# Attention step of a layer kernel: TensorE issues the first pair of scores ahead of the step's first bank of maxima

## What is computed

```
xn  = layernorm(x)
out = x + attention(xn) + experts(xn)

attention: 16 sub-heads of 8 features for q and k, 8 heads of 16 features for v
  q = rope(xn Wq.T) * 8**-0.5,  k = rope(xn Wk.T),  v = xn Wv.T
  probs = softmax(q k.T)                      # 16 x 1024 x 1024 per batch
  diff  = probs[even] - lam * probs[odd]
  y     = rms_normalise(diff v) * (1 - 0.36) ; y Wo.T
experts: 3 of 8 zones per batch, chosen by a router on the mean token:
  sum of w[e] * gelu(xn Wa[e]) Wb[e]
```

## Time and profile before

| | us |
|---|---|
| median of 3 runs | 438.38 (437.73 to 438.41) |
| the profiled execution | 437.34 |
| its span, first to last instruction | 435.6 |
| TensorE busy | 413.3 |
| VectorE busy | 384.4 |
| ScalarE busy | 338.8 |

### The profile page before, as it was taken

One profiled execution on the slowest core, in us unless ns is written; L12 is line 12 of the kernel. 1 busy time (PEld: TensorE's weight loads), 2 busy tenths in 40 slices (PEclk: granted clock), 3 DMA queues, 4 the chain that ended last, 5 costly groups with the idle time before them and its releaser, 6 DMA issues.

```text
span 435.6 us, 7697 instructions
## 1 busy us (share of the span) xinstructions
PE 413.3 (95%) x2742; PEld 185.1 (42%) x2742; DVE 384.4 (88%) x743; ACT 338.8 (78%) x450; POOL 141.4 (32%) x172
## 2 busy tenths in 40 slices
PE   8899999999999899999999999999999999999983
PEld 6665556655565333333332333333333333345542
DVE  4995999999999899999999999899999998888476
ACT  3786565555554799989889989989989899888971
POOL 4269999878763500111020010120121210000002
PEclk9999999999999999999999999999999999999998
DMA  8736751400000150020002063000000000000003
GB/s 273 289 97 216 242 199 47 140 9 1 3 0 3 29 216 0 13 87 3 2 3 98 1 150 49 1 2 2 2 3 0 3 0 4 2 2 2 4 0 96
DMA packets 21871, 24.94 MB, mean 57 GB/s; under 512 B 11818, under 2 KB 16106, under 8 KB 21578
## 3 DMA queue, kind: packets, MB, share of 16 engines
q1 hardware_dynamic: 21096, 23.60, 17.1%
q10 hardware_dynamic: 738, 0.86, 0.7%
HBM read 14.49 MB, written 8.65 MB: 53 GB/s over the span
## 4 chain that ended last, share of the span: by engine, by line
PE 62%; ACT 13%; DVE 13%; issue 9%; DMA 1%; POOL 1%; ACTq 0%; POOLq 0%; DVEq 0%
PE ps L1399 17%; PE ps L1252 16%; ACT E L795 10%; PE ps L1362 10%; DVE part_max L905 6%; PE ps L1324 4%; PE ps L1177 3%; PE ps L1179 3%; PE ps L1178 2%; PE ps L1325 2%; PE ps L1326 2%; PE ps L1390 1%; DMA X<-in_x 1%; PE ps L1380 1%; DVE stats L859 1%
## 5 line engine op out<-in xcount | busy, mean ns | idle before, releaser
L905 DVE TENSOR_REDUCE part_max<-ps 128x1 f32<-128x512 f32 x512 | 319.9, 680 | 28.7 <-PE ps L1252 24.6
L795 ACT ACTIVATE E<-ps 128x1024 f32<-128x1024 f32 x256 | 245.4, 1029 | 32.3 <-PE ps L1362 27.6
L1399 PE MATMUL ps<-E,Vg 128*32 128x512 f32 x896 | 119.3, 604 | 0.1
L1252 PE MATMUL ps<-K,Q 32*128 32x512 f32 x384 | 111.4, 473 | 0.6
L1252 PEld LDWEIGHTS ps<-K,Q 32*128 32x128 f32 x384 | 46.7, 182 | 84.7 <-DVE part_max L905 76.0
L1362 PE MATMUL ps<-Q,K 32*128 32x512 f32 x320 | 77.9, 480 | 4.7 <-ACT E L795 3.1
L559 POOL TENSOR_TENSOR hL<-h,hH 128x512 fp32r<-128x512 f32 x48 | 61.2, 1284 | 11.6 <-ACT hH L763 11.4
L761 ACT ACTIVATE h<-ps 128x512 f32<-128x512 f32 x48 | 28.8, 599 | 32.1 <-PE ps L1179 21.7
L1252 PE MATMUL ps<-xnL,xnH 32*128 32x512 f32 x128 | 44.2, 464 | 0.6 <-DVE part_max L905 0.4
L1362 PEld LDWEIGHTS ps<-Q,K 32*128 32x128 f32 x320 | 32.6, 181 | 25.4 <-ACT E L795 23.3
L610 POOL TENSOR_TENSOR U<-AT,rsum 128x256 f32<-128x256 f32 x15 | 9.3, 621 | 104.2 <-DVE rsum L1057 104.2
(11 more groups left out here) (166 smaller groups left out, 397.3 us busy)
## 6 DMA issues: line engine op xcount, KB each, us to landing
K<-k_scr SPq DMA_DIRECT2D x5, 512.0 KB, 4.2
Q<-q_scr SPq DMA_DIRECT2D x5, 512.0 KB, 6.1
tab<-in_tables SPq DMA_DIRECT2D x2, 1024.0 KB, 10.1
wa_raw<-in_wa SPq DMA_DIRECT2D x6, 256.0 KB, 2.7
wb_raw<-in_wb SPq DMA_DIRECT2D x6, 256.0 KB, 2.9
Q<-max_turned SPq DMA_DIRECT2D x80, 2.0 KB
X<-in_x SPq DMA_DIRECT2D x2, 512.0 KB, 7.0
k_scr<-V SPq DMA_DIRECT2D x2, 512.0 KB, 11.1
```

The costliest lines, as they stand in the source:

```text
L795: nc.scalar.activation(E[:, par, 2 * jj:2 * jj + 2, :].rearrange("p j t -> p (j t)"), ps[:, 2 * jj:2 * jj + 2, :].rearrange("p j t -> p (j ...
L905: nc.vector.tensor_reduce(part_max[:, tile // FC % 2, j * FC + tile % FC, sh:sh + 1], ps[:, SLOT_BANK[x], :], AX.X, ALU.max).then_inc(slot ...
L1252: mm(ps[:, SLOT_BANK[x], :], Qs[g % KQ_BUFS][strip(j), tile % TB * P:(tile % TB + 1) * P], Ks[g % KQ_BUFS][strip(j), sh * BANK:(sh + 1) * ...
L1399: last = mm(ps[QUAD * j:QUAD * (j + 1), B_PV, :], Vg[:, par, st, j // 2, :], E[:, s % 2, k, :], start=(st == 0), stop=(st == TB - 1), skip ...
```

## The change

In a step the first bank of maxima moves from ahead of the first pair of scores to behind it. The first pair of scores, with its waits for the maxima's rows and for the exponent, now stands directly behind the products with V of the step before; then come two banks of maxima, the second pair of scores, and the rest as before. No instruction is added or removed on any engine. If the step's first bank has a quarter's transpose behind it, this moves along.

```diff
@@ -1442,8 +1442,6 @@
             for s in range(ALL_STEPS):
                 nxt = s + 1
                 made = max_slots(s)
-                for t, k in made[:1]:
-                    max_slot(t, k)
                 if nxt < ALL_STEPS:
                     if nxt < QUARTERS_FROM and nxt % TB == 0:
                         pe.wait_ge(qmax_in, half_in(nxt // TB))
@@ -1451,7 +1449,7 @@
                         pe.wait_ge(qmax_in, half_in(2 * GROUPS - 2 + (nxt - QUARTERS_FROM) // QUARTER_STEPS))
                     pe.wait_ge(exp_done, 2 * s + 1)
                     scores(nxt, 0)
-                for t, k in made[1:2]:
+                for t, k in made[:2]:
                     max_slot(t, k)
                 if nxt < ALL_STEPS:
                     pe.wait_ge(exp_done, 2 * s + 2)
```

## The result

The changed kernel takes 435.32 us (median of 6 runs, 433.93 to 436.3), the kernel before 438.31 in the runs beside it: a ratio of 0.9925, 95% interval 0.9906 to 0.9945. That is 3.0 us less, where 1.5 was forecast: faster as said, within the range, and twice the size.

The account below looks back on a forecast made before the run. ScalarE and VectorE, both over nine tenths busy, and TensorE wait for each other; the loop closing last bounds the kernel. Terms -1.0 + 0.4 - 0.9 = -1.5 us on 438.38 give 436.9, range 433.6 to 440.0.

Parts of the forecast that it names:

- the leg from K0 to K2: Step with first bank k=0 to the one with k=2, two steps on: 4.12 us with the change, 4.01 by exponents.
- The two chains: Interleaved exponents over steps with first bank k=0/k=2 and k=1/k=3: four steps take 8.46 and 8.43 us, 8.26 once changed.
- That TensorE passes a blocked product: In the attention loop, a later product starts ahead of one held up by its strip; a conflict costs 0.33 us.
- VectorE's idle time does not fall: Sign of being right, in the attention loop: VectorE waits as long as before; no size given.
- the term of steps 0 to 97: Main part of the loop, 24.5 rounds of four steps at 0.04 us: -1.0 us, bounds -4.7 and +3.7.
- stepping through: Working steps 75 to 88 and 8 to 16 with the taken durations: 0.05 and 0.09 us ahead.
- Steps with four banks: Steps 0, 16 and 81, and step 104's transpose: later first banks push back the products, +0.4 us (0 to +0.8).
- Steps from 98 on: Steps 98 to 121, fewer banks, and step 116's exponent 0.6 us earlier: together -0.9 us (-1.7 to -0.3).
- Pays in full: Rival, whole loop: the ring of three banks absorbs VectorE's lateness, exponents set the pace; about 433.2 us, chance 0.15.
- VectorE becomes the bound and it gets slower: Rival, first reduction of steps with first bank k=0 or k=1: 0.24 us late, 0.09 covered; 440.5 us, chance 0.17.
- Nothing moves: Rival, attention loop: later steps wait for the second exponent, so an earlier first pair gains nothing; 438.4 us, chance 0.13.
- program order: Rival, steps with first bank k=0: TensorE keeps strict order, so four rounds of 0.33 us become three; 433 us, chance 0.03.

Follow-up runs that it names:

- short reduction: First reduction of steps 0 to 97 with first bank k=0 cut to 256 of 512 columns: 432.83 us on the changed kernel, 438.15 on the kernel before.
- each part alone: The move made only in steps with first bank k=0, only k=1, or only k=2 and k=3, against the kernel before: 438.03, 438.00, 438.69 us.
- the banks reordered: Order of a step's banks changed where the first is k=0 or k=1 (steps 1 to 96): 431.05 us on the changed kernel, 431.94 on the kernel before.

## Why the prediction was right, and where it was small

**Right**: the place of the gain (two scores that shared a strip with the first bank), its size for one exponent (0.57 after the pair for the 0.59 taken), and that a late first bank gives VectorE a new bound: 0.77 for its start, 4.13 for 4.12 for the leg from K0 to K2. The two chains' worked times, 8.46 and 8.43, are in the trace as 8.47 and 8.44. The short reduction shows that bound to be real in the changed kernel and absent in the one before.

**That TensorE passes a blocked product** went in as a reading of the earlier trace rows. The Trainium skill, "TensorE: Matmul & The Clock Gate", The mechanism, has matmuls in strict order instead. The changed kernel gives nothing for the other reading: its K1 step has scores and the bank of k = 2 at 307.87 and 307.88, although the bank of k = 1 stands ahead of that one in the program and must wait for its strip.

**One sign was wrong.** "VectorE's idle time does not fall" was named as a sign of being right; it fell by 2.9 us, from 17.4 to 14.5. In a stretch with the same work in it, idle time falls by what the stretch gets shorter, here 242.90 to 240.03, so this sign contradicted the forecast of a gain.

**The step that was mis-sized** is the term of steps 0 to 97, -1.0 us. The working gave 0.09 us per four steps as the gain at best, and I took 0.04 because VectorE would be late by its other work. Measured from copy to copy, steps 8 to 95 gained 1.66, and 0.39 more without the four-bank steps' loss: 2.05 in 22 rounds, 0.093 a round; in the plain blocks it was 0.12 (0.94 in eight rounds). With steps 0 to 7 (0.25) and steps 96 and 97 (0.20, by the exponents' starts) the term comes to -2.5.

Two things were wrong in it. VectorE's transposes did not add to the leg: in the plain blocks' K0 steps that have them it took 4.07 to 4.15. And 0.59 us from pair to exponent in every step, with "in K3 and K2 steps nothing changes", left out the 0.03 by which an exponent starts earlier when its pair is issued first; K2 to K0 takes 4.22 for the 4.25 worked out. The 0.04 came from stepping through, which gave 0.05 us in steps 75 to 88 and 0.09 in 8 to 16; the exponents' starts in the traces give 0.21 and 0.24. Which of the durations used made that difference is not shown.

**Steps with four banks**, +0.4: measured 0.39, but nearly all in steps 16's, 32's and 49's blocks; step 81, the one from which the term was read, shows 0.03. So the size was met in part by luck.

**Steps from 98 on**, -0.9: they gained 1.0, by the exponents' starts. The last block gained 0.81 of it, of which step 116 0.45 where 0.6 was said; the block before it gained nothing. Sum: -2.5 + 0.4 - 1.0 = -3.1, beside the loop's 3.2.

**The rivals.** *Pays in full* asked for 4.01 from K0 to K2; it is 4.13. It would have needed VectorE's lateness absorbed, and the short reduction shows that it was not: it freed another 2.1 us. *VectorE becomes the bound and it gets slower*: the place was right, the price was not, since K0 to K2 grew by 0.12 (4.02 to 4.14) and K2 to K0 fell by 0.23. *Nothing moves* and *program order*: neither; the exponent moved, by 0.19 in K1 steps.

## What to carry to other kernels

Where small products share TensorE's rows in strips, ask of every pair of neighbours in program order whether they use the same strip; a conflict held the second product up by 0.33 us here and the exponent behind it by 0.17 to 0.20, and reordering by strips brought 8.6 us where moving one product brought 3.0. Where two chains run interleaved over one engine, cutting one of them can show nothing until the other is cut too, so a part that is worth nothing alone is not proof against the whole. When a product is moved back to free one engine, work out its other reader's start as well: here it became the new bound and took back about 2 us. And do not take an engine's idle time as a sign for or against a gain when its work stays the same: it falls by whatever the whole gains.

## What was not expected of the hardware

The granted clock fell to half for some 3 us just ahead of the loop in one profiled execution of the changed kernel and not in another (spans 433.6 and 432.2); TensorE had been busy for 1.93 of 2 us before. Neither its cause nor what decides it is shown: the kernel before was busy for the same 1.93 of 2 us there and kept full clock. Five of the thirteen traces have the fall, four of them on other kernels of this family. It is worth 1.2 to 1.4 us, nearly half of the effect that was to be measured, and the loop's own time was 287.3 in both. The blocks of eight steps repeated within 0.04 us over these two executions, where the whole time of the changed kernel ranges over 2.5 us in its runs.

There is a second such place behind the loop. From the last copy of the products to the end it takes 31.4 us in the traces of the kernel before and of the changed one, and 32.3 in those of each part alone and of the banks reordered, both before and changed. In the latter the clock is at half from about 26 us after that copy, in the former from 28 to 29 us. Whether the earlier fall is what makes the end longer is not tested; the blocks of steps 8 to 119 hold neither.
